# First attention of a gated two-layer network: the order of three TensorE steps within a slot, and stage borders without a queue drain

## The reference

```python
x = x + tanh(g_xattn[0]) * L0_xattn(layernorm(x), ctx)     # 16 heads of 16; ctx is 16 x 375 x 256
x = x + tanh(g_ffn[0])   * L0_ffn(layernorm(x))            # 14 routed experts, 2 shared
x = x + tanh(g_xattn[1]) * L1_xattn(layernorm(x), ctx)     # one head of 256
x = x + tanh(g_ffn[1])   * L1_ffn(layernorm(x))            # 4 experts, top 2
# L0_xattn: q, k, v = projections with bias; softmax(q k^T / 4) v per head; then @ Wo + bo
```

## Time and profile before

| | |
|---|---|
| median of 3 runs | 902.34 us (899.74 to 905.33) |
| the profiled execution | 901.96 us, of which its span 900.2 us; some 1.8 us lie around it |
| busy | PE 724.2, DVE 602.7, POOL 483.8, ACT 476.4 us |
| granted TensorE clock | 0.912 on average (1.0 is 2.4 GHz, 0.5 is 1.2 GHz) |
| first attention | from 0 to some 293 us |

### The profile page before, as it was taken

How to read it: one execution, slowest core, us unless ns; L and a number is a source line. 1 busy time by engine, 2 the same in 40 slices (tenths; PEclk the granted TensorE clock), 3 DMA queues, 4 the chain that set the end, 5 groups by cost and what they waited for, 6 DMA issues and landing times. The chain is left out here.

```text
span 900.2 us, 21152 instructions
## 1 busy us (share of the span) xinstructions
PE 724.2 (80%) x6870; PEld 553.6 (62%) x6903; DVE 602.7 (67%) x1448; ACT 476.4 (53%) x969; POOL 483.8 (54%) x608
## 2 busy tenths in 40 slices
PE   3878999999896698989999995787677378998730
PEld 2445666666665698987777774677576246675520
DVE  6665777777776589865555444786876166667766
ACT  3544766676654656853333332446553147776632
POOL 5896789798500538860000006868765417656555
PEclk9997999999999599999999996888889579999985
DMA  6344444433200547861222213686331114323233
GB/s 172 93 101 124 105 112 132 103 102 93 58 15 2 170 134 242 267 217 62 83 83 83 80 57 109 172 224 171 111 103 38 46 54 122 103 83 95 82 93 102
DMA packets 87664, 98.96 MB, mean 110 GB/s; under 512 B 17260, under 2 KB 77132, under 8 KB 87564
## 3 DMA queue, kind: packets, MB, share of 16 engines
q1 hardware_dynamic: 63468, 66.10, 25.0%
q0 software_dynamic: 16432, 24.66, 10.4%
q10 hardware_dynamic: 7664, 6.89, 2.6%
HBM read 61.03 MB, written 24.38 MB: 95 GB/s over the span
## 5 line engine op out<-in xcount | busy, mean ns | idle before, releaser
L783 DVE TENSOR_REDUCE a_mx<-ps 112x2 f32<-112x750 f32 x128 | 120.2, 939 | 51.7 <-PE ps L401 50.1
L673 POOL DMA_DIRECT2D a_stkK<-a_KS x248 | 119.3, 489 | 21.0 <-issue 15.0
L643 ACT ACTIVATE a_Pf<-ps 125x672 f32<-125x672 f32 x128 | 90.1, 729 | 15.9 <-PE ps L345 14.8
L51 PE MATMUL ps<-f_w2hi,f_hh 128*128 (+1 forms) x292 | 80.4, 275 | 4.1 <-issue 2.9
L51 PE MATMUL ps<-f_w2lo,f_hh 128*128 (+1 forms) x292 | 80.3, 275 | 0.0
L51 PE MATMUL ps<-f_w2hi,f_hl 128*128 (+1 forms) x292 | 80.3, 275 | 0.0
L1844 POOL MEMSET a_half<- 112x2 f32 x1 | 0.1, 95 | 143.9 <-POOLq L89 143.9
L2474 POOL TENSOR_TENSOR f_rl<-f_rf,f_rh 128x512 bf16<-128x512 f32 x34 | 39.5, 1162 | 63.6 <-DVE f_rh L2542 63.1
L1548 DVE CAST f_hh<-ps 128x512 bf16<-128x512 f32 x41 | 28.4, 692 | 64.2 <-PE ps L1284 64.2
L2418 ACT ACTIVATE f_rf<-ps,f_ln 128x128 f32<-128x128 f32 x136 | 54.6, 452 | 26.3 <-PE ps L2369 26.3
L1208 POOL DMA_INDIRECT f_xd<-xn,pos x32 | 54.5, 1703 | 22.7 <-issue 22.7
(11 more groups left out here) (397 smaller groups left out, 2336.7 us busy)
## 6 DMA issues: line engine op xcount, KB each, us to landing
a_raw<-F_w SPq DMA_DIRECT2D x22, 512.0 KB
f_xg<-f_xd SPq DMA_DIRECT2D x75, 128.0 KB
f_yd<-f_yo SPq DMA_DIRECT2D x75, 128.0 KB
f_raw<-F_w SPq DMA_DIRECT2D x14, 512.0 KB
a_ctxF<-ctxT SPq DMA_DIRECT2D x16, 375.0 KB
a_cR<-ctx SPq DMA_DIRECT2D x16, 375.0 KB
a_stkK<-a_KS POOLq DMA_DIRECT2D x248, 23.4 KB, 2.0
a_cT_first<-ctxT SPq DMA_DIRECT2D x14, 375.0 KB
```

Of the source, the lines that this page charges most:

```text
L51: ins = nc.tensor.matmul(out, l, r, start=first and i == 0, stop=last and i == len(steps) - 1)
L643: nc.scalar.activation(Pf[:, j % PB], psST[:C, j % 2, :, 0:SC * T], ACT.Exp, scale=DH ** -0.5).then_inc(exp_done, 1)
L673: pool.dma_start(stkK[SIDE * h + DH * a:SIDE * h + DH * (a + 1), w.slot, jj], KS[2 * DH * jj + DH * h:2 * DH * jj + DH * (h + 1), w.odd, p ...
L783: nc.vector.reduce_max(mx[:, n.odd, j // JJ, :, j % JJ], maxima_of(n, j)[:T, :, :S], AX).then_inc(mx_red, 1)
```

## The change

Within a slot PE's order becomes: in odd slots V, M, S; in even slots S, M, then TM, the projection and TV. TM of slot 0 moves behind S. All six `Block()` calls get `no_gpsimd_drain=True`: at the end of a block the other engines have a plain drain, POOL has none, and the barrier is of semaphores alone. `release` loses its first barrier, and its second one becomes one of semaphores alone.

```diff
     def release(self):
-        self.nc.all_engine_barrier()
         self.nc.clear_and_free_semaphores(self.sems)
-        self.nc.all_engine_barrier()
+        self.nc.all_engine_barrier(sem_only=True)
         self.sems = []
...
-        with nc.Block() as block:
+        with nc.Block(no_gpsimd_drain=True) as block:
...
                 def emit(p, b, n, ws, x, l):
                     for s in range(NJ):
-                        if n is not None:
-                            maxima(n, s)
-                        if b is not None and s == 0:
-                            turn_maxima(b, 1)
                         of, j = scores_at(p, b, s)
                         row, g = values_at(p, b, s)
                         if row is not None and s % 2 == 1:
                             values(row, g, row.b * NJ + NJ if of is None else of.b * NJ + j)
-                        if of is not None:
+                        if of is not None and s % 2 == 0:
                             scores(of, j)
+                        if n is not None:
+                            maxima(n, s)
+                        if of is not None and s % 2 == 1:
+                            scores(of, j)
+                        if b is not None and s == 0:
+                            turn_maxima(b, 1)
                         if n is not None and s == 4:
                             turn_maxima(n, 0)
```

## The result

The changed kernel takes 944.36 us (median of 4 runs, 941.87 to 946.03) against 903.84 for the kernel before (4 runs, 899.74 to 906.91). The ratio is 1.0452, with a 95% interval of 1.0409 to 1.0495: slower, as forecast, but by 40.5 us where I gave 26. 944 lies 6 us above the range of 918 to 938.

What follows compares the result with a forecast made beforehand. It took the first attention to be bound by PE and DVE waiting for each other, PE's work nearly filling the round trip. Order +31 us, borders -4.7, sum +26: 928.5 us, range 918 to 938.

Steps and rivals of the forecast that it cites:

- up to turn 3: First attention, turns 1 and 2, which partly wait for transfers: 3 us slower, between bounds of 0 and 4.9.
- The turn: First attention: V lengthens intervals from even slots, odd ones stay 1.40; +2.43 us a turn, 26.7 over 11 turns.
- rival 2: First attention: only the round trip binds, DVE waits in even intervals melt; +13 - 4.7, 910 to 911 us; 4 in 100.
- Rival 3: First attention: V fills PE's waits before TV and TM, M's wait is PE's own pace; faster, 879 us; 3 in 100.
- The clock: First attention: PE busy some 80% of a turn, so granted clock stays full, 2.4 GHz, as in 800 to 862 us.
- Rival 4: First attention: clock falls, PE at half clock in half of the turns, 48 us more, 976 us; 3 in 100.
- the clock shows 0.5 in the turns: Sign of being wrong: granted clock of 0.5 between 82 us and the end of the first attention's turns.
- Turns 14 and 15: End of first attention: output projections in slots 4 to 7 hide the order's cost, slots 0 and 2 pay; 1.2 us.
- The borders: Stage borders: dropped drain and barrier save 0.4 us at the first two, 3.9 at the third; -4.7, bounds -2.4 and -5.3.
- Rival 1: First two borders: the clear's own drain inherits POOL's 6.4 + 3.3 us, third gains nothing; +39.5, 942 us; 9 in 100.

Runs made afterwards that it cites:

- the shorter reduction: New order with the borders of before, DVE's reduction of the maxima over half of the keys: 911.05 us; same edit in the kernel before: 890.49 us.
- the filled kernels: New order with the borders of before, matmuls of S issued two times (944.0 and 936.48 us) or three times (939.17 us) in odd slots.
- S twice: New order with the borders of before, matmuls of S issued two times in odd slots, same result: 944.0 us, 1.0463 to before; second look 936.48 us.

## Why the prediction was wrong

The profiled executions averaged (three of before, two of after) differ by 39.4 us, 13 more than the 26.3 of the sum. By the prediction's own terms:

| term | forecast | measured | from |
|---|---|---|---|
| up to turn 3 | 3 | 1.5 | 87.2 to 88.8 |
| turns 3 to 13 | 26.7 | 35.5 | 151.3 to 186.8 |
| turns 14, 15 and the first border | 1.2 - 0.4 | 6.0 | 57.9 to 63.9 |
| second stage | -0.4 | 1.2 | 252.2 to 253.4; varies by more |
| third stage with its border | -3.9 | -5.4 | 172.2 to 166.8 |
| fourth stage | 0 | 0.6 | 179.7 to 180.3 |

**The turn: right.** 2.43 us a turn were forecast, and where the clock holds it is 2.51. The 0.08 between them is the interval from slot 0, 2.83 where I gave 2.75; the other seven came as worked out. That M of an even slot is the round trip is shown by the shorter reduction; rival 2 had the even intervals melt, and they did the opposite. Rival 3 fell with it.

**The clock: the step that failed.** "So I leave it at the full clock." The schedule alone makes the eleven turns 178.9 us, which the filled kernels show; the changed kernel took 185.4 and 188.3. So 8 of the 8.8 us missed there are stretches at 1.2 GHz. Rival 4 named the mechanism, and priced it at half of the turns at half clock, 48 us, with 3 in 100; what came is a stretch of 3.4 us in four and in six places, each worth some 1.5 to 1.6. That the clock shows 0.5 in the turns was also one of the prediction's own signs of being wrong. The fault is in the argument. I took the busy share of a stretch, 80% in 800 to 862 us at clock 1.00, for what the clock goes by. Here the profile's share does not tell the two cases apart: 144.39 of 178.90 us, 81%, with S twice and no dip, and 7.16 of 9.20, 78%, in the changed kernel just ahead of one; a whole turn of the changed kernel at the full clock (turn 5) has 13.08 of 16.24 us, 81%, as well. What differs is the number of matmuls (2420 against 2161) and the waits between them. The rule in the Trainium skill (TensorE: Matmul & The Clock Gate, "A second HAM failure mode: psum-queue depth-cycling") that I had weighed and set aside agrees with the runs: frequent short waits, and a clock that goes back and forth. The price here is 8 us in eleven turns.

**Turns 14 and 15: wrong in size.** Where the clock holds, slots 0 to 7 of turn 14 take 2.9, 1.4, 2.36, 1.4, 3.22, 1.47, 1.99 and 1.5 us, 16.2 against 15.0 before, and the first seven of turn 15 14.7 against 12.9: 3 us, not 1.2. "There the order costs nothing" nearly holds: slots 4 to 7 of turn 14 take 8.18 us against 8.21, and slots 4 to 6 of turn 15 0.6 more, of which the V after the last M gives 0.2 back. What was mis-summed is "only slots 0 and 2 pay, some 0.6 each: 1.2". That is one turn, and two turns pay it: slots 0 to 3 measured 1.25 more in each, 2.5 together. The other 3 of the 6.0 are clock again, as far as the slots allow a split. With the 8 in turns 3 to 13 the clock then makes some 11 of the 13 us that the sum missed.

**The borders: right.** -4.7 was forecast; the run with the borders alone gives -3.5 by its ratio (-6.3 to -0.7). At the third border, last scatter to first load:

```profile
760.97 0.95 POOL L1831 DMA_INDIRECT f_xd<-xn,f_pos  x1 [0.30 <-issue]
...
763.54 0.82 SPq L2333 DMA_DIRECT2D f_xg<-f_xd  x2
...
765.51 0.29 PEld L2355 LDWEIGHTS ps<-ident,f_xg 128*128 128x128 f32 x2 [9.11 <-DMA f_xg<-f_xd]
```

2.57 us instead of 6.54, so 3.97 earlier, where I gave 3.9 between bounds of 1.6 and 4.5; PE's first transposition follows 4.54 after that scatter instead of 8.55. Rival 1 was half right: a part of POOL's drain is work of its own, as it said, but the drain ahead of the clear is not of that kind. That the measured 944 is near its 942 is chance: none of the 9.7 us that it put at the first two borders came.

**What stays open.** Why the dips sit in slot 4 of some turns and not of others was not settled, nor what of the filling counted, the hole between the two S or the wait before M. The 3 us of clock in the last turns rest on slots picked out where the clock held, not on a run. Nor did filling help there: from turn 14 to the end of the first border the three filled executions took 63.4 to 66.8 us, the order alone 65.1 in both. So that the waits bring the clock down is shown for turns 3 to 13 only.

## What to carry to other kernels

Before moving a filler from one gap to another, write down for each gap what ends it. A gap that ends with another engine's round trip takes work for nothing; one that ends with PE's own work pays in full, and V (0.71 us) was moved from the first kind to the second. Then ask of a PE that will newly wait in each turn what the clock does, and don't answer it with the busy share of another stretch: allow for dips in the range. And take more than one profiled execution before giving a stage a difference of 5 us.

## What the hardware showed that I had not expected

- Matmuls added into a wait can make a stage shorter: 264 more in eleven turns took the stretch from 186.9 and 186.2 to 180.5 and 178.9 us by keeping the clock at 2.4 GHz.
- POOL's drain at the end of a block takes 6.6 us (first stage) and 3.5 us (second) with at least 41 us of nothing before it, and ends 4.0 us after the last scatter's issue instruction in the third. The drain ahead of the clear takes 0.19 and 0.12 us and at the third border of the changed kernel ends within 0.2 us of that issue.
- The second stage, which no edit but those to the borders touched, took between 250.1 and 257 us, and the granted clock went with it.
